# Three DMA and weight-preparation duties moved between engines in a pre-LN attention + RWKV-FFN kernel

## The reference

```python
# x: (8, 4096, 1024) f32, all weights 1024 x 1024
h = layernorm(x)
q, k, v = h @ Wq.T + bq, h @ Wk.T + bk, h @ Wv.T + bv
scores = q @ k.T / sqrt(1024)
masked = where(causal, abs(scores), -inf)       # scores * sign(scores)
x = x + softmax(masked) @ v @ Wo.T + bo
h = layernorm(x); h_prev = shift_by_one_token(h)
xr = mu_r * h + (1 - mu_r) * h_prev
xk = mu_k * h + (1 - mu_k) * h_prev
out = x + sigmoid(xr @ W_r.T) * (square(relu(xk @ W_k.T)) @ W_v.T)
```

## Time and profile before

| | us |
|---|---|
| two runs | 5040.34 and 5412.33, median 5226.33 |
| the profiled execution | 5043.46 |
| its span, slowest core (core 3) | 5041.9 |
| spans of the other cores | 5023.1 to 5041.3 |
| granted TensorE clock, all cores | 0.936 to 0.940 of full speed |

### The profile page before, as it was taken

One profiled execution on the slowest core, in us unless ns is written; L12 is line 12 of the kernel. 1 busy time (PEld: TensorE's weight loads), 2 busy tenths in 40 slices (PEclk: granted clock), 3 DMA queues, 4 the chain that ended last, 5 costly groups with the idle time before them and its releaser, 6 DMA issues.

```text
span 5041.9 us, 64641 instructions; the slowest of 8 cores (5023.1 to 5041.9 us)
## 1 busy us (share of the span) xinstructions
PE 4163.6 (83%) x24576; PEld 2388.1 (47%) x24576; DVE 1594.1 (32%) x3641; ACT 475.4 (9%) x1056; POOL 926.7 (18%) x892
## 2 busy tenths in 40 slices
PE   1999999999568986899877999987758888888888
PEld 0444444444234432444433444443336767777776
DVE  2233333322232232122332232323244444434442
ACT  2000000000010111011100111110111111111111
POOL 4222222222111001110002101100442112121211
PEclk7999999999779987999989999998979999999999
DMA  5111111111443114311216021121430101101010
GB/s 156 51 59 60 63 61 60 43 44 51 131 114 54 34 34 123 44 34 34 66 35 125 9 67 34 34 56 45 76 100 26 51 35 43 51 26 51 26 43 18
DMA packets 187473, 285.93 MB, mean 57 GB/s; under 512 B 19360, under 2 KB 126112, under 8 KB 186656
## 3 DMA queue, kind: packets, MB, share of 16 engines
q1 hardware_dynamic: 102688, 197.89, 13.3%
q10 hardware_dynamic: 50688, 67.13, 3.7%
q0 software_dynamic: 33792, 16.78, 3.2%
HBM read 197.84 MB, written 100.66 MB: 59 GB/s over the span
## 4 chain that ended last, share of the span: by engine, by line
PE 73%; DVE 12%; issue 4%; POOL 4%; ACT 2%; DMA 2%; DVEq 2%; SPq 1%; ACTq 0%; POOLq 0%
PE ps_b L108 12%; PE ps_a L108 12%; PE ps_d L108 11%; PE ps_d L134 11%; PE ps_c L134 11%; PE ps_c L108 10%; DVEq L99 1%; DVE o_sb L1104 1%; DVE ploT L1070 1%; POOL plo L1045 1%; DVE of L825 1%; PE ps_c L120 1%; DVE at_bk L1216 1%; ACT p_sb L1035 1%; SPq L73 1%
## 5 line engine op out<-in xcount | busy, mean ns | idle before, releaser
L1045 POOL TENSOR_TENSOR plo<-p_sb,phi 128x512 bf16<-128x512 f32 (+3 forms) x144 | 154.4, 1072 | 1587.0 <-DVE phi L1039 1587.0
L134 PE MATMUL ps_d<-vhiT,phiT 128*128 128x512 bf16 x544 | 222.6, 409 | 49.3 <-DVE ploT L1070 49.3
L474 POOL TENSOR_TENSOR qk_l<-qk_f,qk_h 128x512 bf16<-128x512 f32 x128 | 147.6, 1153 | 561.2 <-DVE qk_h L468 561.2
L134 PE MATMUL ps_c<-vhiT,phiT 128*128 128x512 bf16 x512 | 202.4, 395 | 48.7 <-DVE ploT L1070 48.7
L716 POOL TENSOR_TENSOR xr_lo<-xrf,xr_hi 128x256 bf16<-128x256 f32 x128 | 86.3, 674 | 844.8 <-DVE xk_hi L710 844.8
L108 PE MATMUL ps_a<-khiT,qhiT 128*128 128x512 bf16 (+2 forms) x576 | 203.6, 358 | 42.1 <-DMA vloT<-svl 42.1
L134 PE MATMUL ps_d<-vloT,phiT 128*128 128x512 bf16 x544 | 223.1, 410 | 0.0
L108 PE MATMUL ps_a<-yT_hi,wq_hi 128*128 128x512 bf16 x256 | 105.2, 411 | 142.1 <-POOL yT_lo L399 60.5
L134 PE MATMUL ps_d<-vhiT,ploT 128*128 128x512 bf16 x544 | 221.6, 407 | 0.0
L108 PE MATMUL ps_b<-khiT,qhiT 128*128 128x512 bf16 (+1 forms) x576 | 211.6, 367 | 0.0
L108 PE MATMUL ps_b<-kloT,qhiT 128*128 128x512 bf16 (+1 forms) x576 | 211.6, 367 | 0.0
(11 more groups left out here) (244 smaller groups left out, 9737.3 us busy)
## 6 DMA issues: line engine op xcount, KB each, us to landing
khiT<-skh SPq DMA_DIRECT2D x160, 128.0 KB, 3.9
kloT<-skl SPq DMA_DIRECT2D x160, 128.0 KB, 3.9
vhiT<-svh SPq DMA_DIRECT2D x80, 256.0 KB, 5.6
vloT<-svl SPq DMA_DIRECT2D x80, 256.0 KB, 5.8
sx<-x SPq DMA_DIRECT2D x32, 512.0 KB, 14.7
sx<-at_bk POOLq DMA_DIRECT2D x64, 256.0 KB, 4.6
xin<-sx SPq DMA_DIRECT2D x32, 512.0 KB, 4.3
x1c<-sx SPq DMA_DIRECT2D x32, 512.0 KB, 4.3
```

The source lines that it names most:

```text
L134: e.matmul(o, ww, mm, start=s, stop=sp),
L474: e.tensor_tensor(d, s, h, op=OP.subtract), inc="gv")
L1045: e.tensor_tensor(d, s_, h, op=OP.subtract), inc="gv")
```

## The change

Three edits, independent of each other:

1. `load_kv(0, 0)` is issued from POOL's queue. POOL waits for the stores of stage A as SP does.
2. In group 0 the other key/value load, `load_kv(0, 1)`, is issued from ACT's queue. Its place in the builder's order is unchanged. Groups 1 to 3 keep SP.
3. The W_r pieces in slots 1 to 8 of the last output projection use `weight_piece` (cast on DVE, subtraction one half on POOL and one on DVE). `weight_piece_sg` is deleted.

```diff
-    def weight_piece_sg(...):      # SP load; ACT cast; POOL subtracts both halves
-        ...
-    def load_kv(g, j):
+    def load_kv(g, j, q="sync"):
         par = j % 2
-        p.wait("sync", kv_busy[par])
+        p.wait(q, kv_busy[par])
...
-        kv_toks[(g, j)] = p.dma_group("sync", prs)
+        kv_toks[(g, j)] = p.dma_group(q, prs)
 
     tok_q_next = load_q(0)
-    load_kv(0, 0)
+    p.waits("gpsimd", tok_pa_stores)
+    load_kv(0, 0, q="gpsimd")
...
                 if (g, jn) not in kv_toks:
-                    load_kv(g, jn)
+                    load_kv(g, jn, q="scalar" if g == 0 else "sync")
...
                 if (g, jn3) not in kv_toks:
-                    load_kv(g, jn3)
+                    load_kv(g, jn3, q="scalar" if g == 0 else "sync")
...
-                        weight_piece_sg(wd["wr"], wr_hi, wr_lo, stgD,
-                                        stg_c2, stg_s2, slot - 1)
+                        weight_piece(wd["wr"], wr_hi, wr_lo, stgD,
+                                     stg_c2, stg_s2, slot - 1)
```

More of the change, by code:

```diff
@@ L263, in load_weight @@
         return copy_toks[:] + sub_toks[:]
[L265 to L286, removed]
     def load_weight_sg(wdram, whi, wlo, stg, copy_toks, sub_toks):
```

## The result

| | before | changed |
|---|---|---|
| median of all runs, us | 5128.4 (33 runs) | 5195.43 (36 runs) |
| fastest run | 5039.8 | 5046.21 |
| ratio, 95% interval | | 1.0019 (1.0010 to 1.0027) |

In many executions of either kernel the cores of one die ran at a lower clock and took up to 14% longer; the ratio leaves these out, and so it doesn't follow the two medians. From 5043.46 it gives + 9.6 us (5 to 14), about 5053 us. The change makes the kernel 0.2% slower, where 2% was named as the size to tell.

The account below looks back on a forecast made before the run. PE, holding 73% of the chain that ended last, was taken as the bound, so edits count only where PE waits. Against 5043.46 us, - 5 + 8 + 0 = + 3 for the three edits gave 5046 us, range 5025 to 5065.

Parts of the forecast that it names:

- the last of the sum: Whole kernel: 5046 us is for executions like the profiled one; the 5412.33 us run, pulling the median to 5226.33, set aside.
- It ends at 1289.5 in either order.: Seam between stages A and B: 9.44 MB at 300 GB/s take 31.5 us from about 1258, whichever load comes first.
- the lower bound of the term: Seam, first key/value load from POOL: a gain of at least 0.5 us, if SP's bytes come last.
- rival 2: Key/value loads: ACT's as slow as in the seam, POOL's gains 0.5; +13 us, 5056, or 5065 if POOL's late; chance 0.12.
- The even share: Seam: POOL's and SP's queues share evenly; POOL's 4.19 MB end at 1286, SP's 5.24 MB at about 1289.5.
- the 18 us that the queue alone would promise: Seam: by SP's issue time alone, the Wo loads issued at 1266 in place of 1284.2 would gain 18 us.
- rival 1: Key/value loads: SP's bytes come first and ACT's load is quick; up to -17 + 0, 5026 us; chance 0.25.
- Rival 4: Seam: DVE's casts of the first two Wo pieces hold up POOL's DMAs; +3 us at most, 5049; chance 0.05.
- Rival 3: Seam: POOL's DMAs go one after the other, up to 5.9 us each; 5152 us with ACT's load; chance 0.03.
- twice that: Pair 8 of group 0: at the lower clock after long idle, its scores take 1.5 us more than 1.5 us.
- rival 5: Last output projection: the W_r pieces on DVE stall PE; +19 us, 5065; chance 0.04.

Follow-up runs that it names:

- Edit 2 alone: Only the second key/value load of group 0 moved to ACT's queue, against the kernel before the change: ratio 1.0016 (1.0004 to 1.0027).
- edit 1 alone: Only the first key/value load moved to POOL's queue, against the kernel before the change: ratio 1.0018 (1.0001 to 1.0036).

## Why the prediction was right or wrong

**The number.** I said 5046 and a range of 5025 to 5065. The reported median, 5195.43, is outside. The step that failed here is the last of the sum: the two runs shown had already a median of 5226.33, and I set it aside as something that the trace doesn't show, so that the range holds for a different number than the one reported. By the ratio the change costs + 9.6 us, so 5053: inside, with the right sign, and three times the + 3 forecast. That it is inside is partly luck: the forecast added a gain that doesn't exist to a loss that was put too high.

**Edit 1 is the term that was wrong: - 5 forecast, + 3.6 measured.** Three things in its step failed.
- The reference point. The prediction measured from a first cast at 1292.10, which is + 41.1 on that core. The other seven cores of the same trace have it between + 36.6 and + 39.4. I had read one core, the slowest, and it was slow at exactly this place. A gain "from 41.1 to 36.5" was mostly the difference between that core and its neighbours.
- "It ends at 1289.5 in either order." The bytes are the same, but with two queues the last landing is 5 to 6 us later, whichever queue the second is (+ 42.8 from POOL, + 43.4 from ACT, + 37.6 before). So the lower bound of the term, a gain of 0.5 us, excluded what happened; only rival 2 allowed for a late load in its upper end of 5065. Nothing in the trace of before had two full queues side by side, and that should have made a loss one of the bounds.
- The even share. It was even in packets and not in bytes: 2.63 MB for POOL and 1.67 for SP in 15 us. POOL had issued everything by + 17.6, SP was held back, and q and Wo came last. I named "if the cast is near 1292 again, my even share was wrong" as the sign of it.

What held is that SP's queue was not the limit. The sentence of the Trainium skill that I weighed (DMA: Bandwidth & Descriptors, Issuing engines are not separate DMA queues) points the right way, against the 18 us that the queue alone would promise. The trace agrees that nothing was gained, and shows a loss besides. POOL's issue was priced at 1.3 us for each DMA from an accumulating one, and is 0.54 (24 in 13 us), off by more than two. POOL was never late by it; but rival 1 counted on an issue spread over 20 to 31 us to give SP more than an even share, and SP got less. Rival 4, DVE holding up POOL's DMAs, can't be judged: POOL had issued its last DMA 26 us before the first cast, so the two never met. Rival 3, one DMA after the other, is excluded by the same rows.

The Wo chain itself (24.5 us on that core, 23.2 from first to last cast as the median) became 21.2 us, 2 less, where I had under 1 for the competitor that leaves. Edit 2 alone, which takes it away, gives 22.2, and edit 1 alone, which doesn't, 21.8; why the chain is shorter behind edit 1 isn't shown. By the shorter chain + 5.0 at the first cast is only + 2.8 at the exponential.

**Edit 2: + 8 forecast, + 5.3 measured.** The mechanism was right. The prediction's own terms give 10.7 - 3.4 + 1 = 8.3, and its "twice that" for the scores would have been 1.5 and not 1. Each link is in the rows: ACT issues 24 DMAs behind exponential 4, in 12.6 us (1366.72 to 1379.3) where I took 13.05 and a landing of 5.8; the stall is 9.11 us on core 5 where I had 10.7; and pair 5 gets back 2.6 us (from the scores of pair 8 to the product of pair 5 it is 4.24 us, 6.86 before), where I had 3.4 less 1. The scores of pair 8 took 2.5 us (1384.92 to 1387.42, granted clock 0.50) in place of 1.5, so 1 us it was. That leaves 6.5 us on this core (6.1 by the two moments there). The mis-sized term is the stall: of its 1.6 us, 0.7 are the load, from first issue to the scores 18.2 us in place of 18.9, and the rest its start, as ACT's first issue goes out 0.10 us after exponential 4 has started, and not behind its end.

**Edit 3: 0 forecast, 0 measured.** The slots keep their length, DVE's gap shrinks by 1.4 us, and rival 5 is out.

## What to carry to other kernels

When a sum is made of terms of a few us, read each of its starting points on all cores first; a spread of 4 us between cores swallows a term of 5. A second queue was no extra road where the DMA engines were busy: here it decided which transfer came last, by the size of the packets, and the last came 5 us later. So ask which transfer the critical chain waits for before any load is moved. And a load that is moved to a compute engine inherits that engine's place in the order: here 24 issues behind one exponential made PE wait 9 to 12 us, while the place on SP behind the Wo loads was free.

## What was unexpected

- POOL's issue wasn't held back: 0.54 us for each of its plain DMAs of 128 and 256 KB at a DMA share of 1.00, while the sixteen q loads on SP stretch from 8.9 to 15.5 us beside them (median of the cores; 22.7 on the slowest).
- Two queues shared the DMA engines evenly by packets. POOL's packets were 1.6 times as large as SP's and ACT's half as large, and the bytes went the same way.
- With two queues the last of 9.44 MB lands about 5 us later than with one, with the DMA share down to 0.17 in the last 5 us (median of the cores).
- 4.19 MB from a second queue beside loads of 512 KB, two at a time, made the longest wait of DVE for such a load 4.5 to 11.4 us on four cores, in place of at most 3.8.
